# New instruction orders on four engines in the last stage of a two-block gated decoder kernel

## The chip, the cores and the metric

The kernel runs on one core of one Trainium2 chip. Its time is the device time of one execution in microseconds (us); a row of figures is given as the median of several runs. Lower is better. Five engines run their own instruction streams side by side and meet at semaphores: TensorE (PE) multiplies matrices, VectorE (DVE) and ScalarE (ACT) work on rows, GpSimd (POOL) issues the indexed gathers and does a little arithmetic, SyncE (SP) issues most other transfers. An instruction that has to wait holds up everything behind it on its engine.

## The reference, cut to what matters

```
x = x + tanh(g_xattn[0]) * xattn(layernorm(x), ctx, ctx, mask)      # cross attention, 77 keys
x = x + tanh(g_ffn[0])   * moe(layernorm(x))                        # 8 experts, top 2, plus a shared expert
x = x + tanh(g_xattn[1]) * L1_xattn(layernorm(x), ctx, ctx)         # softmax over the queries
x = x + tanh(g_ffn[1])   * L1_ffn(layernorm(x))
# L1_ffn: h = silu(x @ wg.T) * (x @ wu.T);  out = h @ wd.T          # hidden width 768, int weights / 127
```

x is 4 batches of 1024 rows of 256 numbers in float32. `L1_xattn` normalizes its softmax over the 1024 queries of a batch, so a batch has to be complete before its output can be formed.

## The kernel before, in words

Rows are cut into 8 groups `u` of 512 (4 tiles of 128 rows, `GT` = 4), two groups to a batch (`GB` = 2). The first stages (attention, routing, experts) fill the first 420 us. The last stage computes, group by group, the tail of the expert layer, `L1_xattn` and `L1_ffn`, and writes the output. This text calls one pass of `for b in range(B)` a turn; there are four. Turn `b` runs `L1_ffn` of batch `b` (groups `2b` and `2b+1`, called its first and second half here, `c` = 0 and 1) and, woven in, all that batch `b+1` needs before it.

The names in the code, with their engine:

- `up3(b, c, m)` on TensorE: block `m` of six of gate and up products, 8 matmuls into two banks. `down3(b, c, False)` and `down3(b, c, True)`: blocks 0 to 3, then 4 and 5, of the product with `wd`. The first of these calls works on tiles 0 and 1, then waits for the product of block 5 and works on tiles 2 and 3.
- `hidden3` on ScalarE issues for block `m` a silu (L1008, into one of three buffers `sl`), and then the high part `g3h` (L699). On VectorE `hidden3` is the gated product, silu times up (L2155), in place; `low3` is the low part `g3l` (L2160), product minus high part. The next silu in the same buffer waits for that low part. `up3` of block `m` waits for the gated product of block `m-2`, since it writes the same banks.
- For batch `b+1`: `gather` on GpSimd (L624, 8 indexed DMAs per group, two to a tile) fetches expert rows; `x2` on VectorE (L2077) adds them in, 8 instructions per group; `stats3` (L2086, L2089), `rstd3` on GpSimd (L633, L637), `shift3` (L2102) and `norm3` on ScalarE (L961) are the layer norm; `t3` (L1554) transposes, `copy_n3` copies to SBUF, `scores3` (L1562) multiplies with the keys, `score_max` and `softmax3` follow, `out3` (L1571) forms the output, `residual3` adds it, `stats4`, `norm4`, `t4` (L1580), `copy_n4` and `n4_low` make the input of `up3`, and `final` (L2169) forms the result.

The order of work on each engine is written out by hand; there is no scheduler. On GpSimd `paced(b, c, j, m)` issues the gather of tile `j` only once `m` gated products are done. On every engine the order of the code is the order in which work is issued.

## Time and profile before

| | |
|---|---|
| median of 3 runs | 638.63 us (636.67 to 639.14) |
| span of the profiled execution | 657.9 us |
| TensorE busy | 607.1 us, 92% |
| VectorE busy | 443.4 us, 67% |
| ScalarE busy | 363.6 us, 55% |
| GpSimd busy | 250.0 us, 38% |
| mean granted TensorE clock | 0.979 |

The times of the three runs are device times of executions without a profile; the profile is of another execution, whose span is 19.3 us longer than the median. No other time of the profiled execution is recorded beside its span. The four turns of the last stage lie at about 469.9 to 523.1, 523.1 to 571.7, 571.7 to 619.8 and 619.8 to 657.9 us of the span. Busy time on TensorE is the union of modelled matmul times; a back-to-back matmul starts about 0.23 us after the one before but is shown as 0.39 us long, so a gap in the stream of starts is about 0.16 us longer than the idle time that the profile shows.

### The profile page before, as it was taken

To read this page: it belongs to the slowest core of one execution; us is meant where nothing else is said; L and a number is where in the kernel's file an instruction comes from. 1 tells how busy PE (TensorE), PEld (TensorE's weight loads), DVE (VectorE), ACT (ScalarE), POOL (GpSimd) and SP (SyncE) were. 2 spreads that over 40 slices of the span, in tenths; PEclk is the share of its full clock that TensorE was granted. 3 is DMA by queue.
4 is the path that set the end of the run, shared out by engine and by line. 5 is a ranking of instruction groups with operands and counts; after the bars stand their busy time and mean duration, and the time that the engine had idled before them with its cause. 6 is when DMAs were issued, how large, how long until landed. Compare 5 with 4: busy or idle time off the path is not lost.

```text
span 657.9 us, 12684 instructions
## 1 busy us (share of the span) xinstructions
PE 607.1 (92%) x3562; PEld 498.5 (76%) x3562; DVE 443.4 (67%) x1321; ACT 363.6 (55%) x806; POOL 250.0 (38%) x315
## 2 busy tenths in 40 slices
PE   8889999888986999999999999699879989999997
PEld 6667777776755788888888888586757867877886
DVE  3988888864653666666666663467876796866755
ACT  5687778855532555555555543155654674674643
POOL 4345564434352336232323236567442732200000
PEclk9899999988898999999999999899999999999999
DMA  6335664454063953333333317532111331100000
GB/s 199 126 126 180 220 204 160 164 167 143 25 256 120 321 162 106 105 106 105 105 107 105 106 57 260 204 117 71 49 49 48 101 108 48 49 1 32 33 33 33
DMA packets 46657, 77.53 MB, mean 118 GB/s; under 512 B 7604, under 2 KB 31615, under 8 KB 46335
## 3 DMA queue, kind: packets, MB, share of 16 engines
q1 hardware_dynamic: 38521, 57.55, 26.3%
q0 software_dynamic: 7344, 19.14, 8.7%
q8 instruction: 33, 0.54, 0.3%
q14 instruction: 33, 0.27, 0.1%
q10 hardware_dynamic: 726, 0.02, 0.1%
HBM read 44.52 MB, written 32.17 MB: 117 GB/s over the span
## 4 chain that ended last, share of the span: by engine, by line
PE 52%; DVE 18%; issue 9%; ACT 7%; DMA 4%; POOL 4%; another core or an unknown queue 4%; SPq 1%; ACTq 0%; DVEq 0%; POOLq 0%
PE bank L1162 11%; PE bank L1164 10%; PE bank L1163 10%; PE bank L1602 5%; PE bank L1623 3%; PE bank L1624 3%; PE bank L1464 2%; PE bank L1455 2%; DMA rows_by_expert<-n,pos 2%; DVE xa L2077 2%; DVE st L2086 2%; PE bank L1562 2%; DVE sl L2155 1%; DVE xa L2138 1%
## 5 line engine op out<-in xcount | busy, mean ns | idle before, releaser
L582 POOL TENSOR_TENSOR yg<-yg,b 128x256 f32<-128x256 f32 x71 | 52.3, 737 | 115.7 <-ACT yg L699 115.7
L2038 DVE TENSOR_TENSOR hb<-bank,b 128x512 f32<-128x512 f32 x71 | 49.1, 692 | 59.4 <-PE bank L1164 59.1
L536 POOL DMA_INDIRECT rows_by_expert<-n,pos x64 | 65.6, 1025 | 61.2 <-DVE pos L1890 44.7
L1602 PE MATMUL bank<-n4Th,wint 128*128 128x512 f32 x192 | 74.6, 409 | 5.5 <-DVE sl L2155 4.1
L624 POOL DMA_INDIRECT yr<-expert_out,out_row x64 | 66.7, 1042 | 20.4 <-issue 17.4
L699 ACT ACTIVATE hTh<-bank 128x256 fp32r<-128x256 f32 x71 | 27.3, 384 | 82.0 <-PE bank L1464 82.0
L1602 PE MATMUL bank<-n4Tl,wint 128*128 128x512 f32 x192 | 71.9, 395 | 0.0
L699 ACT ACTIVATE g3h<-sl 128x512 fp32r<-128x512 f32 x60 | 37.8, 631 | 45.5 <-DVE sl L2155 32.0
L1162 PE MATMUL bank<-w13h,xTh 128*128 x142 | 56.4, 397 | 0.2 <-DVE xTl L2045 0.2
L1164 PE MATMUL bank<-w13h,xTl 128*128 x142 | 56.0, 394 | 0.0
L1163 PE MATMUL bank<-w13l,xTh 128*128 x142 | 55.8, 393 | 0.0
L1162 PE MATMUL bank<-n2Th,wsh 128*128 128x256 f32 (+1 forms) x128 | 44.3, 346 | 9.2 <-DVE n2Tl L1819 3.3
L1623 PE MATMUL bank<-wint,g3h 128*128 128x256 f32 x192 | 48.2, 292 | 2.4 <-issue 1.4
L1602 PEld LDWEIGHTS bank<-n4Th,wint 128*128 128x128 f32 x192 | 35.4, 188 | 17.8 <-DVE sl L2155 8.6
L2155 DVE TENSOR_TENSOR sl<-bank,sl 128x512 f32<-128x512 f32 x48 | 32.9, 686 | 23.3 <-ACT sl L1008 23.3
L1162 PE MATMUL bank<-w2h,hTh 128*128 x142 | 45.8, 323 | 0.3 <-DVE hTl L2042 0.3
L1624 PE MATMUL bank<-wint,g3l 128*128 128x256 f32 x192 | 46.0, 281 | 0.0
L633 POOL TENSOR_SCALAR ve<-mv 128x4 f32<-128x4 f32 x16 | 6.0, 377 | 102.7 <-DVE mv L2089 97.0
L1602 PEld LDWEIGHTS bank<-n4Tl,wint 128*128 128x128 f32 x192 | 36.0, 188 | 8.0
L1163 PE MATMUL bank<-n2Tl,wsh 128*128 128x256 f32 (+1 forms) x128 | 41.6, 325 | 0.0
L1164 PE MATMUL bank<-n2Th,wsl 128*128 128x256 f32 (+1 forms) x128 | 41.3, 323 | 0.0
L961 ACT ACTIVATE n<-xa,nb,rs 128x256 f32<-128x256 f32 x64 | 34.2, 595 | 10.7 <-DVE nb L2102 10.7
(299 smaller groups left out, 1787.6 us busy)
## 6 DMA issues: line engine op xcount, KB each, us to landing
xg<-rows_by_expert SPq DMA_DIRECT2D x71, 128.0 KB, 2.1
expert_out<-yg SPq DMA_DIRECT2D x71, 128.0 KB, 1.7
stage<-in_wexp SPq DMA_DIRECT2D x24, 256.0 KB
x_shared<-x SPq DMA_DIRECT2D x8, 512.0 KB
xa<-x_shared SPq DMA_DIRECT2D x4, 1024.0 KB
out<-ost SPq DMA_DIRECT2D x8, 512.0 KB, 2.6
xin<-in_x SPq DMA_DIRECT2D x7, 512.0 KB, 5.1
wint<-in_wint POOLq DMA_DIRECT2D x3, 768.0 KB, 10.7
```

The lines of the kernel that those rows point to most:

```text
L536: pool.indirect_dma_start(out=xs, out_offset=bass.IndirectOffsetOnAxis(ap=pos[p][:, k, j:j + 1], axis=0), in_=n2[p][:, j, :], in_offset=No ...
L582: pool.tensor_tensor(yg[s], yg[s], b2[:, bass.ds(e, 1), :].rearrange("p a d -> p (a d)"), ALU.add)\
L624: pool.indirect_dma_start(out=yr[:, c, k, j, :], out_offset=None, in_=ys, in_offset=bass.IndirectOffsetOnAxis(ap=out_row[:, b * GB + c, k, ...
L699: return act.activation(dst, src, ACT.Copy)
L1162: mm(o, ah, bh, start=first, stop=False)
L1163: mm(o, ah, bl, start=False, stop=False)
L1164: return mm(o, al, bh, start=False, stop=final)
L1602: last = mm(bank[:, 2 * (m % 2) + w, :], wt[:, k, m * P:(m + 1) * P], part[c][:, k, :], start=(q == 0 and k == 0), stop=(q == 1 and k == K ...
L1623: mm(bank[:, j, 0:D], g3h[:, k, t], wdv[:, k, :], start=(k == 0), stop=False)
L1624: last = mm(bank[:, j, 0:D], g3l[:, k, t], wdv[:, k, :], start=False, stop=(k == ML - 1))
L2038: tt(hb[p], bank[:, p, :], b13[:, bass.ds(e, 1), :].rearrange("p a n -> p (a n)"), ALU.add)\
L2155: tt(sl3[n % 3], bank[:, 2 * (m % 2) + 1, :], sl3[n % 3], ALU.mult).then_inc(sem("g3_done"), 1)
```

## The change

The same operations are issued with the same operands; some are cut in halves (two tiles, one bank or one group at a time), and the order on four engines is new. Up to the first turn the order of compute instructions is unchanged on every engine. The core of the diff follows; conditions that hold in the first three turns are left out or joined to their line.

```diff
@@ GpSimd
             paced(2, 0, 3, 1)
+            rstd3(0, 4, "n3_done")
             paced(2, 1, 0, 2)
+            rstd3(1, 2, "n4_done")
             paced(2, 1, 1, 4)
-            rstd3(0, 4, "n3_done")
             paced(2, 1, 2, 6)
-            rstd3(1, 2, "n4_done")
+            rstd3(1, 3, "n4_done")
             paced(2, 1, 3, 8)
             paced(3, 0, 0, 9)
-            rstd3(1, 3, "n4_done")
...
             paced(3, 1, 1, 16)
-            rstd3(0, 6, "n3_done")
+            rstd3(1, 4, "n4_done")
             paced(3, 1, 2, 18)
-            rstd3(1, 4, "n4_done")
             paced(3, 1, 3, 20)
             rstd3(1, 5, "n4_done")
+            rstd3(0, 6, "n3_done")
@@ ScalarE: hidden3 is cut into silu3 (the silu) and high3 (the high part); one turn
+                silu3(b, 0, 0)
+                if nxt: norm3(u, first)
+                if b == 0: copy_n4(1, (0,))
+                high3(b, 0, 0)
+                if b == 0: copy_n4(1, (1,))
+                silu3(b, 0, 1)
+                if nxt: norm3(u, second)
+                silu3(b, 0, 2)
+                high3(b, 0, 1)
+                if nxt: copy_n3(u, (0,)); copy_n3(u, (1,))
+                silu3(b, 0, 3)
+                high3(b, 0, 2)
+                if nxt: norm3(u + 1, first); norm3(u + 1, second)
+                silu3(b, 0, 4)
+                high3(b, 0, 3)
...
@@ TensorE, one turn
                 up3(b, 0, 2)
                 t3(u)
-                for m in range(3, ML): up3(b, 0, m)
-                t3(u + 1)
+                up3(b, 0, 3)
+                up3(b, 0, 4)
+                scores3(b + 1, (0,))
+                t3(u + 1)
+                up3(b, 0, 5)
                 down3(b, 0, False)
-                scores3(b + 1)
+                scores3(b + 1, (1,))
                 down3(b, 0, True)
                 up3(b, 1, 0)
                 up3(b, 1, 1)
-                out3(b + 1)
-                for m in range(2, ML): up3(b, 1, m)
+                out3(b + 1, (0,))
+                up3(b, 1, 2)
+                out3(b + 1, (1,))
+                up3(b, 1, 3)
...
@@ VectorE, second half of a turn
                 hidden3(b, 1, 1)
+                residual3(u, (0,))
                 low3(b, 1, 0)
-                residual3(u)
-                stats4(u)
-                x3_read(u)
-                low3(b, 1, 1)
+                residual3(u, (1,))
+                stats4(u)
+                residual3(u + 1, (0,))
                 hidden3(b, 1, 2)
-                residual3(u + 1)
-                shift3(1, u)
+                low3(b, 1, 1)
+                residual3(u + 1, (1,))
+                shift3(1, u)
                 low3(b, 1, 2)
...
                 hidden3(b, 1, 4)
-                shift3(1, u + 1)
                 hidden3(b, 1, 5)
                 low3(b, 1, 4)
+                shift3(1, u + 1)
```

The line numbers in the next rows are those of the version that each is taken from. First VectorE in the first half of the first turn, before, from the gated product of block 1 to that of block 4 (`sl` in and out: gated product; `g3l`: low part; `xa` from `yr`: the adding of gathered rows; `st` and `mv`: statistics; `nb`: shift).

```order
L2155 TENSOR_TENSOR sl_210<-bank,sl_210 128x512
L2160 TENSOR_TENSOR g3l<-sl_209,g3h 128x512
L2077 SCALAR_TENSOR_TENSOR xa_196<-yr,gate_all,xa_196 128x256 x4
L2086 BN_STATS st_221<-xa_196 128x6 x4
L2089 BN_AGGR mv_223<-st_221 128x2 x4
L2155 TENSOR_TENSOR sl_211<-bank,sl_211 128x512
L2160 TENSOR_TENSOR g3l<-sl_210,g3h 128x512
L2102 SCALAR_TENSOR_TENSOR nb_227<-mv_223,rs_229 128x4
L2155 TENSOR_TENSOR sl_209<-bank,sl_209 128x512
L2160 TENSOR_TENSOR g3l<-sl_211,g3h 128x512
L2077 SCALAR_TENSOR_TENSOR xa_197<-yr,gate_all,xa_197 128x256 x4
L2155 TENSOR_TENSOR sl_210<-bank,sl_210 128x512
```

The same place now, again from block 1's product to block 4's:

```order
L2223 TENSOR_TENSOR sl_210<-bank,sl_210 128x512
L2151 BN_STATS st_221<-xa_196 128x6 x4
L2155 BN_AGGR mv_223<-st_221 128x2 x4
L2228 TENSOR_TENSOR g3l<-sl_209,g3h 128x512
L2223 TENSOR_TENSOR sl_211<-bank,sl_211 128x512
L2228 TENSOR_TENSOR g3l<-sl_210,g3h 128x512
L2168 SCALAR_TENSOR_TENSOR nb_227<-mv_223,rs_229 128x4
L2223 TENSOR_TENSOR sl_209<-bank,sl_209 128x512
L2228 TENSOR_TENSOR g3l<-sl_211,g3h 128x512
L2142 SCALAR_TENSOR_TENSOR xa_197<-yr,gate_all,xa_197 128x256 x2
L2223 TENSOR_TENSOR sl_210<-bank,sl_210 128x512
```

The statistics now stand ahead of block 0's low part, the second pass of `x2(3)` has gone ahead of block 1's product, and block 4's product is behind two instructions of `x2(4)` and no longer behind four.

ScalarE at that place before, from the silu of block 1 to that of block 4 (`sl` from `bank`: silu; `g3h`: high part; `n_201`: norm; `n3T`: copy of the transposed norm):

```order
L1008 ACTIVATE sl_210<-bank 128x512
L961 ACTIVATE n_201<-xa_196,nb_227,rs_229 128x256 x2
L699 ACTIVATE g3h<-sl_210 128x512
L1008 ACTIVATE sl_211<-bank 128x512
L699 ACTIVATE g3h<-sl_211 128x512
L699 ACTIVATE n3T<-bank 128x512 x2
L1008 ACTIVATE sl_209<-bank 128x512
L961 ACTIVATE n_201<-xa_196,nb_227,rs_229 128x256 x2
L699 ACTIVATE g3h<-sl_209 128x512
L1008 ACTIVATE sl_210<-bank 128x512
```

And now:

```order
L1013 ACTIVATE sl_210<-bank 128x512
L966 ACTIVATE n_201<-xa_196,nb_227,rs_229 128x256 x2
L1013 ACTIVATE sl_211<-bank 128x512
L704 ACTIVATE g3h<-sl_210 128x512
L704 ACTIVATE n3T<-bank 128x512 x2
L1013 ACTIVATE sl_209<-bank 128x512
L704 ACTIVATE g3h<-sl_211 128x512
L966 ACTIVATE n_201<-xa_196,nb_227,rs_229 128x256 x4
L1013 ACTIVATE sl_210<-bank 128x512
```

Each silu has moved ahead of the high part of the block before it, and the copies of the transposed norm no longer stand behind block 2's high part.

GpSimd from the first turn on, as a difference (`ve` and `rs` are one `rstd3`, 225 and 229 for the norm of `L1_xattn`, 226 and 230 for that of `L1_ffn`):

```order
-L624 DMA yr<-expert_out,out_row 128x256 x6
-L633 TENSOR_SCALAR ve_225<-mv_223 128x4
-L637 TENSOR_TENSOR rs_229<-ve_225,halfpow 128x4
 L624 DMA yr<-expert_out,out_row 128x256 x2
+L633 TENSOR_SCALAR ve_225<-mv_223 128x4
+L637 TENSOR_TENSOR rs_229<-ve_225,halfpow 128x4
+L624 DMA yr<-expert_out,out_row 128x256 x2
 L633 TENSOR_SCALAR ve_226<-mv_224 128x4
 L637 TENSOR_TENSOR rs_230<-ve_226,halfpow 128x4
```

Four gathers (the tiles 0 and 1 of group 5) that were issued ahead of `rstd3(0, 4)` now come behind it, and two of these behind `rstd3(1, 2)` too.

## Rows read from the trace of the kernel before

**Rows 1.** Busy time by turn: PE, PEld, DVE, ACT, POOL, granted clock, DMA share, GB/s
```profile
469.90:523.10 53.20, 47.79 (x259) 37.77 (x258) 40.16 (x101) 31.33 (x58) 24.72 (x26) 1.00 0.17 53
523.10:571.70 48.60, 46.12 (x250) 36.63 (x249) 38.81 (x98) 29.52 (x55) 15.98 (x18) 1.00 0.23 74
571.70:619.80 48.10, 45.70 (x249) 36.49 (x248) 34.24 (x82) 29.33 (x54) 4.49 (x6) 1.00 0.06 23
619.80:657.90 38.10, 34.22 (x193) 29.08 (x191) 19.95 (x30) 14.74 (x26) 0.00 (x0) 1.00 0.11 42
```
**Rows 2.** Groups by line from 469.9 us on: busy us, mean ns, idle before
```profile
L2155 DVE TENSOR_TENSOR sl<-bank,sl 128x512 f32<-128x512 f32 x48 | 32.9, 686 | 23.3 <-ACT sl L1008 23.3
...
L1008 ACT ACTIVATE sl<-bank 128x512 f32<-128x512 f32 x48 | 28.2, 588 | 18.5 <-DVE g3l L2160 10.0 <-PE bank L1602 8.1
```
**Rows 3.** Timeline, TensorE, first turn: start, length, instruction, [idle before, releaser]
```profile
479.87 0.40 PE L1602 MATMUL bank<-n4Th,wint 128*128 128x512 f32 x1
480.10 0.39 PE L1602 MATMUL bank<-n4Tl,wint 128*128 128x512 f32 x1
481.65 0.50 PE L1602 MATMUL bank<-n4Th,wint 128*128 128x512 f32 x1 [1.16 <-DVE sl L2155]
...
483.40 0.39 PE L1602 MATMUL bank<-n4Tl,wint 128*128 128x512 f32 x1
484.50 0.50 PE L1602 MATMUL bank<-n4Th,wint 128*128 128x512 f32 x1 [0.71 <-DVE sl L2155]
...
486.23 0.39 PE L1602 MATMUL bank<-n4Tl,wint 128*128 128x512 f32 x1
486.73 1.10 PE L1554 MATMUL bank<-ident,n 128*128 128x128 f32 x8
489.20 0.38 PE L1623 MATMUL bank<-wint,g3h 128*128 128x256 f32 x1 [1.37 <-issue]
...
491.08 0.28 PE L1624 MATMUL bank<-wint,g3l 128*128 128x256 f32 x1
491.99 0.38 PE L1623 MATMUL bank<-wint,g3h 128*128 128x256 f32 x1 [0.63 <-DVE sl L2155]
...
497.02 0.68 PE L1623 MATMUL bank<-wint,g3h 128*128 128x256 f32 x1
497.54 0.28 PE L1624 MATMUL bank<-wint,g3l 128*128 128x256 f32 x1
```
**Rows 4.** Timeline, VectorE, first turn
```profile
475.36 1.29 DVE L2149 TENSOR_TENSOR n4Tl<-bank,n4Th 128x512 fp32r<-128x512 f32 x2 [1.30 <-ACT n4Th L699]
...
479.35 1.40 DVE L2086 BATCH_NORM_STATS2 st<-xa 128x6 f32<-128x256 f32 x4
...
480.94 0.66 DVE L2155 TENSOR_TENSOR sl<-bank,sl 128x512 f32<-128x512 f32 x1
481.51 0.68 DVE L2160 TENSOR_TENSOR g3l<-sl,g3h 128x512 fp32r<-128x512 f32 x1
...
486.88 1.67 DVE L2077 SCALAR_TENSOR_TENSOR xa<-yr,gate_all,xa 128x256 f32<-128x256 f32 x4 [1.83 <-DMA yr<-expert_out,out_row]
488.46 0.68 DVE L2155 TENSOR_TENSOR sl<-bank,sl 128x512 f32<-128x512 f32 x1
```
**Rows 5.** Chain that ended last: the landing of that gather (start, length)
```profile
484.06 2.79 DMA yr<-expert_out,out_row
```
**Rows 6.** Timeline, GpSimd, first turn
```profile
481.12 0.23 POOL L633 TENSOR_SCALAR ve<-mv 128x4 f32<-128x4 f32 x1 [8.93 <-DVE mv L2089]
...
508.61 0.57 POOL L633 TENSOR_SCALAR ve<-mv 128x4 f32<-128x4 f32 x1 [9.70 <-DVE mv L2089]
```
**Rows 7.** Who waited for whom, TensorE, second turn: us in total, times, longest
```profile
PE bank L1602 <- DVE sl L2155: 1.1, 2, 0.6
PE bank L1554 <- ACT n L961: 0.4, 1, 0.4
PE bank L1623 <- DVE sl L2155: 0.4, 1, 0.4
```

More of the change, by code:

```diff
@@ L1031, in late_high @@
                 copy(lhh[:, m, :], lsil[m % 2]).then_inc(sem("hh_done"), 1)
+            first, second = range(2), range(2, GT)
             late_silu(0, 0)
@@ L1046, in _ @@
             late_silu(1, 2)
-            norm3(0, range(2))
+            norm3(0, first)
             late_high(1, 2)
-            norm3(0, range(2, GT))
+            norm3(0, second)
             late_silu(1, 3)
@@ L1052, in _ @@
             copy_n3(0)
-            norm3(1)
+            norm3(1, first)
+            norm3(1, second)
             late_silu(2, 0)
@@ L1064, in _ @@
             late_high(2, 3)
-            norm4(0)
-            copy_n4(0)
+            norm4(0, first)
+            norm4(0, second)
+            copy_n4(0, (0,))
+            copy_n4(0, (1,))
             for b in range(B):
@@ new lines, in _ @@
+                silu3(b, 1, 1)
+                high3(b, 1, 0)
+                silu3(b, 1, 2)
+                high3(b, 1, 1)
+                high3(b, 1, 2)
+                silu3(b, 1, 3)
+                if nxt:
+                    norm4(u, first)
+                high3(b, 1, 3)
+                if nxt:
+                    norm4(u, second)
+                silu3(b, 1, 4)
+                high3(b, 1, 4)
+                silu3(b, 1, 5)
+                if nxt:
+                    copy_n4(u, (0,))
@@ L1097, in _ @@
+                high3(b, 1, 5)
+                if nxt:
+                    norm4(u + 1, first)
+                if nxt:
+                    copy_n4(u, (1,))
+                if nxt:
+                    norm4(u + 1, second)
+                if nxt:
+                    copy_n4(u + 1, (0,))
+                if nxt:
+                    copy_n4(u + 1, (1,))
         @block.tensor
@@ L2073, in x2 @@
                 for k in ks:
-                    for j in range(GT):
+                    for j in tiles:
                         if k:
@@ L2205, in _ @@
             late_out(0, 1)
-            stats3(0)
+            stats3(0, first)
+            stats3(0, second)
             late_hidden(1, 1)
@@ L2211, in _ @@
             late_hidden(1, 2)
-            x2(1, (0,))
+            x2(1, (0,), first)
+            x2(1, (0,), second)
             late_hidden(1, 3)
@@ L2215, in _ @@
             late_low(1, 3)
-            x2(1, (1,))
-            stats3(1)
+            x2(1, (1,), first)
+            x2(1, (1,), second)
+            stats3(1, first)
+            stats3(1, second)
             late_out(1, 0)
@@ L2223, in _ @@
             late_low(2, 0)
[L2224 removed]
+            x2(2, (0,), first)
+            x2(2, (0,), second)
+            x2(2, (1,), first)
+            x2(2, (1,), second)
             late_hidden(2, 1)
[L2226 removed]
+            stats3(2, first)
+            stats3(2, second)
             late_low(2, 1)
[L2228 removed]
             score_max(0)
@@ L2231, in _ @@
             late_hidden(2, 2)
-            residual3(0)
+            residual3(0, (0,))
+            residual3(0, (1,))
             late_hidden(2, 3)
-            stats4(0)
+            stats4(0, first)
+            stats4(0, second)
             x3_read(0)
@@ L2238, in _ @@
             shift3(1, 0)
-            residual3(1)
-            stats4(1)
+            residual3(1, (0,))
+            residual3(1, (1,))
+            stats4(1, first)
+            stats4(1, second)
             x3_read(1)
@@ L2279, in _ @@
                 if more:
-                    stats3(u + GB)
+                    stats3(u + GB, first)
+                if more:
+                    stats3(u + GB, second)
                 if nxt:
                     score_max(b + 1)
-                final(b * GB)
+                final(b * GB, (0,))
+                final(b * GB, (1,))
                 if nxt:
```

267 lines of the change are left out of this document (164 added, 103 removed).

## The prediction, made before the changed kernel was run

> **What bounds the kernel now.** I read the busy times by turn first, then the waits of TensorE, then the timelines of the four engines beside each other. In the turns the reader sees TensorE busy for 47.8 of 53.2 us, 46.1 of 48.6, 45.7 of 48.1 and 34.2 of 38.1, at a granted clock of 1.00 throughout, and VectorE for 40.2, 38.8, 34.2 and 20.0 [rows 1]. TensorE is the bound, and its matmuls are the same before and after. So the change can win only what TensorE waits, and that is a few us in each of the first three turns. In the last turn nothing is woven in; its view of waits names none for TensorE, and its 3.9 us without work are the tail behind the last matmul. The share of busy time says nothing more: the question is which of the waits end earlier in the new order.
>
> How long TensorE really stands still I read from starts. Back to back, a matmul of 512 columns starts 0.23 us after the one before it (479.87 and 480.10 in [rows 3]), while it is shown 0.39 us long. So each listed wait is 0.16 us longer in truth, and short ones are not listed. In the first half of the first turn, by the rows:
>
> - before block 4: 481.65 - 480.10 - 0.23 = 1.32 us, for the gated product of block 2;
> - before block 5: 484.50 - 483.40 - 0.23 = 0.87 us, for that of block 3;
> - before the transposes of group 3: 486.73 - 486.23 - 0.23 = 0.27 us, for its norm;
> - before the down product: the eight transposes at 486.73 take about 0.8 us, so 489.20 - 487.54 = 1.66 us, for the product of block 4;
> - in the middle of the down product: 491.99 - 491.08 - 0.12 = 0.79 us, for block 5's [rows 3].
>
> Together 4.9 us. The product of block 4 was late because `x2(4)` ahead of it on VectorE waited 1.83 us for a gather [rows 4], which GpSimd could issue only behind `rstd3(0, 3)`, which waited for the statistics of group 3 [rows 6]. From the start of that `rstd3` at 481.12 to the landing at 484.06 + 2.79 = 486.85 are 5.73 us [rows 5, 6].
>
> **The change part by part, first turn, first half.** VectorE waited 1.30 us for both copies of n4 at 475.36 [rows 4]. Now the first copy stands ahead of block 0's high part on ScalarE, which starts this chain about 0.5 us earlier. The statistics of group 3 also no longer wait for block 0's low part, about 0.6 us (back to back a low part takes 0.6; it is shown as 0.68 [rows 4]). They start about 1.1 us earlier, at 478.3 instead of 479.35. The product of block 2 comes behind them and the low part, so it gains only the 0.5: 480.94 becomes about 480.5. TensorE waits 0.9 instead of 1.32 there: 0.45 won. Block 1's product is now behind all of `x2(3)` and ends at 478.4, just when block 3 wants it: nothing lost, 0.1 at most.
>
> Between blocks 4 and 5 TensorE now has half of the scores (about 1.5 us) and the transposes (0.8). That covers the wait for block 3's product: 0.87 won, and the 0.27 before the transposes goes too, since they come later than the norm is done (about 484.0 against 484.9). `rstd3(0, 3)` starts 1.1 us earlier, so the gather lands at 485.8. Then two instructions of `x2(4)` (1.67 us for four [rows 4], so 0.8) and the product of block 4, 0.69 [rows 2], end at 487.3; TensorE reaches the down product at about 487.7. So the 1.66 us go. But three of the six remaining `x2` pairs are now ahead of block 3's low part, which ends at 489.5, and the down product asks for it 1.4 us after its start, at 489.1: 0.4 lost. Block 5's product ends at 490.1, when the middle of the down product is reached: 0.79 won. Scores in two parts cost one more passage from float32 matmuls to others: the first matmul behind the scores takes 0.52 us to the next start where 0.12 is usual (497.02 and 497.54 in [rows 3]). Bounds are 0 (no gap stands ahead of them, and what follows is now a transpose) and 0.40; I take 0.3, near the row. Sum: 0.45 + 0.87 + 0.27 + 1.66 + 0.79 - 0.4 - 0.3 = 3.3 us.
>
> **Second turn, first half.** Listed waits of TensorE are 1.1 in two places (blocks 2 and 5), 0.4 for a norm and 0.4 in the middle of the down product [rows 7]. The wait ahead of block 2 stays: n4's low parts and four instructions of `x2` stand ahead of block 0's product as before. The norm's wait stays too, as `shift3`, two norm pairs and a silu stand in the same order. Block 5's wait (0.55 + 0.16 = 0.7) goes under scores and transposes, the transposes' own small wait (0.27, as in the first turn) goes, and the one in the down product (0.4 + 0.16, say 0.5) goes, since nothing waits for a gather here. Less 0.3 for the scores: 1.2 us. **Third turn**, the same without the last: 0.7 + 0.27 - 0.3 = 0.7 us.
>
> **Second halves of the turns.** Here TensorE hardly waits. `out3` in two parts costs one more passage (0 to 0.4, I take 0.2), and stands so that the residual of one group overlaps the output of the other; VectorE's norm may be 0.3 us earlier. I take nothing for the three halves together; bounds are a loss of 1.2 (0.4 each) and a gain of 1.8 (0.6 each, were the products never late). **Edits at nothing:** the waits moved into functions, the memsets and the smaller calls before the first turn keep their order, so what lies ahead of 469.9 us stays.
>
> **GpSimd.** A `rstd3` now waits for statistics with gathers queued behind it. `rstd3(0, 4)` holds up two gathers of group 5, and `rstd3(1, 2)` two more. Those come at about 507, the last gather of group 5 lands near 518 and is wanted by `x2(5)` near 521; group 6's eight DMAs end near 527, land near 528.5, and are wanted near 531.5. Both have 3 us in hand, which hides them. If that cover went, each us late would be a us of VectorE ahead of a gated product.
>
> The row that bears on port sharing: the tiny `ve` on GpSimd takes 0.23 us beside a gated product, which reads PSUM, and 0.57 us at 508.61, where VectorE runs a low part with two SBUF inputs [rows 6]. The Trainium skill, "SBUF — State Buffer", section "SBUF: two separate sides", says that a VectorE operation with two SBUF inputs and a GpSimd operation that reads SBUF lock each other out of a shared port pair for a whole instruction; by that rule, the trace agrees, 0.34 us are at stake per `rstd3`, which eats into the 3 us and changes no term.
>
> **Sum.** 3.3 + 1.2 + 0.7 = 5.2 us less. The profiled span would go from 657.9 to 652.7. The runs without a profile are 19.3 us shorter than the span; I carry the difference over in us: 638.63 - 5.2 = **633.4 us**.
>
> **Rivals.**
> (1) *More comes back.* If the remaining waits ahead of blocks 2 and 4 (0.9 in the first turn, 0.7 in the others), the low part's 0.4, and the passages (3 x 0.3) go too, and the second halves give 0.3 each: 5.2 + 0.9 + 1.4 + 0.4 + 0.9 + 0.9 = 9.7, less the norm's part: about 9 us, 629.6. For it: halves let work start early everywhere. Against: VectorE has the same sum of work ahead of those products.
> (2) *The waits are only moved.* The gather lands as late as before (then 0.9 of the 1.66 stays), block 1's product, now behind `x2(3)`, holds up block 3 by 0.5, and both kinds of passage cost their full 0.4 (0.1 more in three scores, 0.4 in three outputs): 5.2 - 0.9 - 0.5 - 0.3 - 1.2 = 2.3 us, 636.3. For it: VectorE is 76% busy in the first turn and each late product costs TensorE at once.
> (3) *Slower: the ring of three silu buffers.* Each high part now waits behind the next block's silu, hence for its matmuls, and the low part comes after it; the silu three blocks on waits for that low part. Three blocks are 3 x 8 x 0.235 = 5.6 us. The chain is one block (1.9), silu 0.59 [rows 2], high part about the same, low part 0.68: 3.8 us. So it decides as soon as more than 1.8 us of other VectorE work stands ahead of the low part; statistics take 1.6. It happens at four places in a turn (two `stats3` or `x2`, two `stats4`), and at 0.7 us each in twelve places it takes 8.4 us and leaves 3.2 us of loss: 641.8. Against it: the margins that I find are 0.2 us and more.
>
> **How the numbers follow.** Forecast, a gain of 3.2 to 7: 0.51. Rival 1, beyond 7: 0.13. Rival 2, within 0.5% (3.2 us, about what a measurement here can tell from no change): 0.27. Rival 3: 0.09. Faster by over 0.5% has the first two, 0.64; same 0.27; slower 0.09. The range runs from 630.0 (rival 1 nearly whole) to 638.3 (all of rival 2 down to no gain; of rival 3 nothing); the forecast's own is 631.5 to 635.5.
>
> **What the changed profile would show.** In the first half of the first turn TensorE waits for no product before block 5 nor before the down product, and the sum of its gaps there is 1.3 to 2 us, not 4.9. The gather of tile 3 of group 4 lands 1 us earlier by the matmuls' own time. Turns two and three are 1.2 and 0.7 us shorter, the fourth unchanged. I am wrong if ScalarE's silus show waits for low parts with TensorE idle beside them (rival 3), if `x2(5)` or `x2(6)` wait for a DMA, or if the second halves move by over 1 us either way.

## The result, and the profile after

| | before | after |
|---|---|---|
| median, same chip | 637.65 us (633.96 to 639.14, 4 runs) | 628.00 us (625.35 to 630.61, 4 runs) |
| ratio | | 0.9842 (0.9809 to 0.9874) |
| span of the profiled execution | 657.9 us | 628.9 us (its own time 630.61) |
| mean granted TensorE clock | 0.979 | 0.997 |

Against 637.65 us the ratio is a gain of 10.1 us (8.0 to 12.2). The forecast was 633.4 us with a range from 630.0 to 638.3: the direction is right, the gain is about twice as large, and the time lies below the range. It lies below rival 1 too, which said 629.6.

The spans of the two profiles differ by 29 us, which is no measure of the change: the profile of before comes from an execution some 20 us slower than the timed ones. Most of it lies ahead of the turns, which begin at 469.9 us before and at 449.1 us after. One place of it is a wait on ScalarE's timeline (before, then after); more on it below.

```profile
423.15 0.69 ACT L1024 ACTIVATE sl<-bank,bs 128x512 f32<-128x512 f32 x1 [13.93 <-remote]
```
```profile
403.65 0.69 ACT L1030 ACTIVATE sl<-bank,bs 128x512 f32<-128x512 f32 x1 [7.38 <-PE bank L1213]
```

The turns themselves can be compared, though only with this one execution: no profile of the kernel before exists from an execution of 637 to 638 us. By the windows of the kernel after (columns as in [rows 1], cut at its own turns):

```profile
449.10:497.80 48.70, 46.16 (x258) 37.68 (x257) 39.24 (x101) 31.69 (x58) 19.74 (x22) 1.00 0.16 47
497.80:544.00 46.20, 44.89 (x250) 36.93 (x249) 38.59 (x99) 29.47 (x54) 20.28 (x22) 1.00 0.27 89
544.00:590.30 46.30, 44.98 (x252) 37.02 (x250) 34.17 (x83) 29.47 (x54) 4.49 (x6) 1.00 0.06 24
590.30:628.90 38.60, 34.24 (x194) 29.33 (x192) 20.48 (x31) 14.73 (x26) 0.00 (x0) 1.00 0.11 42
```

VectorE and ScalarE are busy for as long as before within 2.5%. TensorE's idle time fell from 5.4, 2.5 and 2.4 us [rows 1] to 2.5, 1.3 and 1.3. Its busy time fell too, from 47.8, 46.1 and 45.7 us to 46.2, 44.9 and 45.0, although its matmuls are the same: a short wait behind a matmul is shown as busy, as the next section works out. To see where the time went, I measure each half of a turn from the first `up3` matmul of its block 0 to that of the next half, and t4b, the last, to the start of the last matmul. t1a is the first half of turn 1, t1b the second, and so on. The halves in all tables of this text are such differences of two starts, each from one profile.

| half | t1a | t1b | t2a | t2b | t3a | t3b | t4a | t4b |
|---|---|---|---|---|---|---|---|---|
| before | 29.85 | 23.05 | 25.82 | 22.73 | 25.49 | 22.73 | 17.09 | 17.05 |
| after | 26.60 | 22.14 | 24.07 | 22.15 | 24.09 | 22.14 | 17.09 | 16.91 |
| gained | 3.25 | 0.91 | 1.75 | 0.58 | 1.40 | 0.59 | 0.00 | 0.14 |
| forecast | 3.3 | 0 | 1.2 | 0 | 0.7 | 0 | 0 | 0 |

Together 8.6 us. It lies inside the interval of the measured gain; whether the rest, 1.5 us, is real can't be told. In the profiles of this text from chips as fast as this one, the kernels with this change start their first turn anywhere from 444.8 to 450.0 us.

The timeline of TensorE in the first half of turn 1, after:

```profile
459.24 0.40 PE L1660 MATMUL bank<-n4Tl,wint 128*128 128x512 f32 x1
460.27 0.50 PE L1660 MATMUL bank<-n4Th,wint 128*128 128x512 f32 x1 [0.64 <-DVE sl L2223]
460.61 0.40 PE L1660 MATMUL bank<-n4Tl,wint 128*128 128x512 f32 x1
...
462.24 1.88 PE L1618 MATMUL bank<-n3T,kqT 128*77 128x512 f32 x4
463.95 1.04 PE L1608 MATMUL bank<-ident,n 128*128 128x128 f32 x8
464.74 0.48 PE L1660 MATMUL bank<-n4Th,wint 128*128 128x512 f32 x1
...
468.12 0.28 PE L1682 MATMUL bank<-wint,g3l 128*128 128x256 f32 x1
469.00 0.36 PE L1681 MATMUL bank<-wint,g3h 128*128 128x256 f32 x1 [0.59 <-DVE g3l L2228]
```

Of the five waits in [rows 3] one is left, 460.27 - 459.24 - 0.23 = 0.80 us before block 4 (forecast 0.9), and a new one has come, 469.00 - 468.12 - 0.12 = 0.76 us for a low part in the down product (forecast 0.4). Two waits that the forecast doesn't name are in both kernels: 1.04 us before the transposes of n4 in turn 1, and about 0.5 us ahead of each of the first three second halves. Block 5's wait lies under half of the scores and the transposes. The gather that had held up the product of block 4 is no longer felt, though VectorE waits longer for it than in [rows 4] (timeline of VectorE, after):

```profile
465.18 0.88 DVE L2142 SCALAR_TENSOR_TENSOR xa<-yr,gate_all,xa 128x256 f32<-128x256 f32 x2 [2.96 <-DMA yr<-expert_out,out_row]
465.98 0.68 DVE L2223 TENSOR_TENSOR sl<-bank,sl 128x512 f32<-128x512 f32 x1
466.58 1.67 DVE L2142 SCALAR_TENSOR_TENSOR xa<-yr,gate_all,xa 128x256 f32<-128x256 f32 x4
468.16 0.69 DVE L2228 TENSOR_TENSOR g3l<-sl,g3h 128x512 fp32r<-128x512 f32 x1
```

It starts 16.1 us into the turn instead of 16.95, and two `x2` instead of four stand between it and the product. In all four turns this is the only `x2` that shows a wait for a gather.

### The profile page after: what moved, and what is told of

It reads as the page before. It is cut to its first block, busy times and chain, and to the rows that moved or that the text cites. A ratio compares the mean times of both kernels' runs of the same rounds, so it can differ in the third digit from the quotient of the medians.

```text
span 628.9 us, 12725 instructions
## 1 busy us (share of the span) xinstructions
PE 594.8 (95%) x3562; PEld 493.5 (78%) x3562; DVE 442.4 (70%) x1321; ACT 364.0 (58%) x806; POOL 249.2 (40%) x315
## 4 chain that ended last, share of the span: by engine, by line
PE 56%; DVE 12%; issue 8%; ACT 7%; POOL 7%; DMA 7%; SPq 3%; ACTq 0%; POOLq 0%; DVEq 0%
PE bank L1660 11%; PE bank L1211 9%; PE bank L1213 9%; PE bank L1212 9%; POOL yr L624 3%; PE bank L1681 3%; PE bank L1682 3%; DMA rows_by_expert<-n,pos 3%; PE bank L1513 2%; PE bank L1504 2%; POOL rows_by_expert L536 2%; PE bank L1629 2%; DVE xa L2142 2%; DMA stage<-in_wexp 1%; DVE n2Tl L1882 1%
## 5 line engine op out<-in xcount | busy, mean ns | idle before, releaser
L1211 PE MATMUL bank<-n2Th,wsh 128*128 128x256 f32 (+1 forms) x128 | 42.8, 334 | 9.3 <-DVE x L1894 6.8
L2223 DVE TENSOR_TENSOR sl<-bank,sl 128x512 f32<-128x512 f32 x48 | 33.1, 689 | 26.0 <-ACT sl L1013 25.4
L1681 PE MATMUL bank<-wint,g3h 128*128 128x256 f32 x192 | 47.8, 291 | 0.6 <-DVE g3l L2228 0.6
L1013 ACT ACTIVATE sl<-bank 128x512 f32<-128x512 f32 x48 | 28.3, 589 | 30.9 <-PE bank L1660 30.4
L1212 PE MATMUL bank<-n2Tl,wsh 128*128 128x256 f32 (+1 forms) x128 | 40.2, 314 | 0.0
```

The costliest lines, as they stand in the source:

```text
L1211: mm(o, ah, bh, start=first, stop=False)
L1212: mm(o, ah, bl, start=False, stop=False)
L1681: mm(bank[:, j, 0:D], g3h[:, k, t], wdv[:, k, :], start=(k == 0), stop=False)
```

## What the forecast left out

**Cut operations cost TensorE nothing.** I had charged 0.3 us for scores in two parts and 0.2 for outputs in two. By the starts, scores whole take 497.02 - 493.99 = 3.03 us (before), the halves 463.95 - 462.24 = 1.71 and 472.81 - 471.50 = 1.31 us. The outputs whole take 506.86 - 503.60 = 3.26 us, a half 481.05 - 479.51 = 1.54. First before, then after:

```profile
493.99 3.60 PE L1562 MATMUL bank<-n3T,kqT 128*77 128x512 f32 x8
497.02 0.68 PE L1623 MATMUL bank<-wint,g3h 128*128 128x256 f32 x1
...
503.60 3.62 PE L1571 MATMUL bank<-vob,attnT 97*128 97x256 f32 x16
506.86 0.58 PE L1602 MATMUL bank<-n4Th,wint 128*128 128x512 f32 x1
```
```profile
471.50 1.88 PE L1618 MATMUL bank<-n3T,kqT 128*77 128x512 f32 x4
472.81 0.68 PE L1681 MATMUL bank<-wint,g3h 128*128 128x256 f32 x1
...
479.51 1.89 PE L1629 MATMUL bank<-vob,attnT 97*128 97x256 f32 x8
481.05 0.58 PE L1660 MATMUL bank<-n4Th,wint 128*128 128x512 f32 x1
481.48 0.39 PE L1660 MATMUL bank<-n4Tl,wint 128*128 128x512 f32 x1
```

The first step behind outputs is 0.42 us instead of 0.23, and it now comes twice; but the two pieces take 3.08 us where the whole took 3.26, so the sum is the same. The steps one by one tell why. Inside the scores of before each step is 0.43 us, but from the last score to the down product it is 0.03, and the step behind that is the 0.52 us that I had charged as a cost over the usual 0.12. What is too much in one step is missing in the one before it: the last score's own time is recorded one instruction late. There was no cost, with the scores whole or cut.

**Waits too short for the list.** The view of waits names none for TensorE in the second half of turn 2 behind its first matmul. The timeline of before has them:

```profile
561.31 0.40 PE L1602 MATMUL bank<-n4Tl,wint 128*128 128x512 f32 x1
561.85 0.50 PE L1602 MATMUL bank<-n4Th,wint 128*128 128x512 f32 x1
562.19 0.40 PE L1602 MATMUL bank<-n4Tl,wint 128*128 128x512 f32 x1
562.43 0.39 PE L1602 MATMUL bank<-n4Th,wint 128*128 128x512 f32 x1
...
563.60 0.39 PE L1602 MATMUL bank<-n4Tl,wint 128*128 128x512 f32 x1
563.98 1.09 PE L1580 MATMUL bank<-ident,n 128*128 128x128 f32 x8
564.83 0.36 PE L1623 MATMUL bank<-wint,g3h 128*128 128x256 f32 x1
```

Ahead of block 5 the step is 0.54 us instead of 0.23, ahead of the transposes 0.38. A matmul is shown 0.16 us longer than its step, so a wait under that shows as no idle time, and one of 0.3 us shows as 0.15. Turn 1's second half has the same two, and a third of 0.24 us in the middle of its down product. The kernel after has none of these; in turn 2:

```profile
536.41 0.40 PE L1660 MATMUL bank<-n4Tl,wint 128*128 128x512 f32 x1
536.64 1.04 PE L1638 MATMUL bank<-ident,n 128*128 128x128 f32 x8
537.45 0.38 PE L1681 MATMUL bank<-wint,g3h 128*128 128x256 f32 x1
```

**A wait costs more than itself.** The step behind a late matmul is 0.34 us (561.85 to 562.19, and 460.27 to 460.61) where 0.23 is usual. So each wait that goes gives 0.1 us more. With that t2b closes by rows: 0.31 + 0.10 + 0.15 = 0.56 of the 0.58 us.

## The experiments

The result and the runs below are six comparisons, each within one chip, and they fall in two kinds. In three the kernel before takes 637 to 638 us, in three 652 to 655 us, and there both kernels show long waits of ScalarE, most of which no event in the trace ends. I call those chips the second kind. That it is the chip is not shown, since none was used twice; the profile of before, 657.9 us long, has the signs of the second kind too, though the timed executions beside it took 634 to 639 us. A ratio is always to the kernel before on the same chip, and the halves come from one profile each.

### Is each half its own matter?

*The kernel before as it is.* (second kind)

> The kernel before, once more, for a second profile of it. By turns the first profile of before has 52.90, 48.55, 48.38 and 33.98 us from first matmul to first matmul, the changed one 48.74, 46.22, 46.23 and 34.00: 8.6 us less. Theory: the four turns repeat within 0.2 us each, and the 20.9 us by which the first turn started earlier in the changed kernel's profile (449.1 against 469.9 us) belong to the execution that was profiled (granted clock 0.979 against 0.997): the first turn starts here at 449 to 452. Rival: part of the measured gain, 10 us by the ratio, lies ahead of the turns, and the first turn starts here at 454 or later at a clock like the changed kernel's.

652.0 us; halves 29.82, 23.08, 25.82, 22.73, 25.50, 22.73, 17.09, 17.07. They are those of the first table to 0.03 us, on another chip, so the halves are a good measure. But this execution too is of the second kind. Its first turn starts at 462.3 us, at a granted clock of 0.984, and not at 449 to 452 as the theory had it, nor at a clock like the changed kernel's as the rival had it; so whether part of the gain lies ahead of the turns stays open.

*Old second halves on VectorE, ScalarE and TensorE*, first halves new:

```diff
 TensorE, second half of each turn (VectorE, ScalarE likewise)
-                out3(b + 1, (0,))
-                up3(b, 1, 2)
-                out3(b + 1, (1,))
-                up3(b, 1, 3)
-                up3(b, 1, 4)
-                up3(b, 1, 5)
+                out3(b + 1)
+                for m in range(2, ML):
+                    up3(b, 1, m)
```

> The changed kernel with the old order in the second half of each turn on VectorE, ScalarE and TensorE, the new one in the first half and on GpSimd. Theory (waits of 0.3 to 0.6 us too short for the list of waits were in the second halves and I left them out): the second halves take 23.0, 22.7 and 22.9 us again where the changed kernel has 22.1 each, so 2.2 us are lost: turns of about 49.6, 46.8 and 47.0. Rival (the second halves only profit from an earlier start of their work in the first halves): they stay within 0.2 us of 22.1 each, and under 0.6 us is lost.

646.98 us, ratio 0.9924 (0.9899 to 0.9950) to the kernel before on the chip. First halves 26.53, 24.89, 24.08; second 23.06, 23.07, 22.72: where the order is new the new numbers stay (t2a would be 24.1; see below), and where it is old t1b and t3b return to the old numbers. t2b is even 0.34 us longer than in the kernel before, by a wait of 0.24 + 0.10 us in its down product that the kernel before has in t1b alone. So the theory holds: the second halves' own order gives their gain.

*Old first halves*, the same way round:

```diff
 TensorE, first half of each turn (VectorE, ScalarE likewise)
-                t3(u, (0,)); t3(u, (1,))
-                up3(b, 0, 3); up3(b, 0, 4)
-                scores3(b + 1, (0,))
-                t3(u + 1, (0,)); t3(u + 1, (1,))
-                up3(b, 0, 5)
+                t3(u)
+                for m in range(3, ML):
+                    up3(b, 0, m)
+                t3(u + 1)
                 down3(b, 0, False)
-                scores3(b + 1, (1,))
+                scores3(b + 1)
```

> The changed kernel with the old order in the first half of each turn on VectorE, ScalarE and TensorE, the new one in the second half and on GpSimd. Theory (the halves add up): the first halves take 29.9, 25.8 and 25.5 us again where the changed kernel has 26.6, 24.1 and 24.1, so 6.4 us are lost, and the second halves keep their 22.1 each. Rival (the GpSimd order makes the first turn's gather land early by itself): the first turn's first half stays under 28.5 us with the old orders elsewhere.

652.87 us, ratio 1.0016 (0.9991 to 1.0042). First halves 29.82, 29.68, 25.20; second 22.21, 22.14, 22.13. t1a is back at its old length, so GpSimd's new order did not bring the gather early by itself. And t1b's 0.9, t2b's 0.6 and t3b's 0.6 us belong to the second halves' own order, for which I had put nothing. t3a gets 0.3 us of its 1.4 from them too. But t2a is 3.9 us longer than in the kernel before, and that eats the gain of the others.

### Which engine's order?

*Old order on TensorE alone*, everything else new (both pieces above, on TensorE only):

> The changed kernel with TensorE's old order in all turns, the other three engines new. Theory (cover: what counts is that scores, transposes and half outputs stand where TensorE used to wait for a gated product): more than half of the 8.6 us is lost, 4.5 to 7 us; TensorE waits again ahead of blocks 2 and 5 of a first half and before the down product. Rival (what counts is that the products come earlier on VectorE and ScalarE): under 2 us is lost, and the waits for products stay short though nothing covers them.

656.59 us, ratio 1.0072 (1.0048 to 1.0096). Halves 28.30, 22.67, 32.35, 22.66, 24.98, 22.63. Against the kernel after, TensorE's own order is worth 1.70 us in t1a, 0.53 in t1b, 0.51 in t2b, 0.89 in t3a and 0.49 in t3b: half to nine tenths of what each gained, and 4.1 of 6.7 us together. That is under the 4.5 to 7 us of the theory for all halves, but t2a, disturbed, can't be counted; the rival, under 2 us, is out. The rest comes from products that are ready earlier. The view of waits of this kernel for t1a names the wait for block 4's product ahead of the down product again, shown as 1.6 us where it was 1.37 [rows 3]:

```profile
PE bank L1681 <- DVE sl L2213: 1.6, 1, 1.6
PE bank L1638 <- ACT n L966: 0.9, 1, 0.9
PE bank L1660 <- DVE sl L2213: 0.6, 1, 0.6
PE bank L1681 <- DVE g3l L2218: 0.6, 1, 0.6
```

*Old order on GpSimd alone.* The edit is the GpSimd part of the change, undone from `paced(2, 0, 3, 1)` on; its first lines:

```diff
             paced(2, 0, 3, 1)
-            rstd3(0, 4, "n3_done")
             paced(2, 1, 0, 2)
-            rstd3(1, 2, "n4_done")
             paced(2, 1, 1, 4)
+            rstd3(0, 4, "n3_done")
             paced(2, 1, 2, 6)
+            rstd3(1, 2, "n4_done")
...
```

> The changed kernel with GpSimd's old order. Theory (GpSimd's order has slack either way, the other engines make the gain): all halves within 0.2 us of the changed kernel's. Rival (a gather queued ahead of a norm's power now delays that norm): rstd3 of the second norms comes later and the second halves of turns one and two take 0.5 us or more longer.

651.28 us, ratio 0.9941 (0.9905 to 0.9976); halves 26.62, 22.27, 29.55, 22.14, 24.08, 22.14. GpSimd's order moves no half (t2a, 29.55, is disturbed here as in the changed kernel beside it). The 3 us that I had counted in hand for its gathers were enough.

*The same together with old first halves:*

> The changed kernel with the old order in the first half of each turn on VectorE, ScalarE and TensorE, and the old order on GpSimd. With GpSimd's new order turn two's first half took 29.7 us, of which ScalarE stood 5.0 us ahead of a copy of n4 with nothing in the trace to end that wait. Theory (the ten gathers in a row of GpSimd's new order, beside the load of a batch, hold up what ScalarE waits for): with the old order it goes, and turn two's first half takes 25.8 us. Rival (the wait has another cause and stays): 28.5 us or more.

One run, 657.15 us; halves 29.84, 22.29, 30.30, 22.14, 25.20, 22.14, those of old first halves alone but for the disturbed one. That one stays, so GpSimd's new order is not what disturbs it: the theory falls and the rival holds.

### Why is the gain smaller on the second kind of chip?

*The changed kernel as it is*, three more times:

> The changed kernel once more, on a chip whose runs of before stand beside it. Theory (the gain is made in the turns and is the same everywhere): halves of 26.6, 22.1, 24.1, 22.2, 24.1, 22.1, 17.1 us within 0.1 each, and 8.6 us less than before, a ratio of 0.986 to 0.987. Rival (waits that no event of the trace ends, as the 5.0 to 5.6 us on ScalarE ahead of the copies of n4 in two of the mixed kernels, also hit the changed kernel on such a chip): one half is 2 us or more longer and the ratio is over 0.990.

> The changed kernel as it is, as the measure for the three kernels beside it. Both theories expect what it showed on the chip where the kernel before took 655 us: the first half of turn 2 near 30.5 us instead of the 24.07 of its first profile, the wait without an event (some 5 us, ahead of ScalarE's copy of the group-3 transposes) in it, and a stretch of about 7 us at the lower granted clock of TensorE behind it. Where the kernel before takes under 640 us, both expect 24.1 us there and no such wait. Time against the kernel before: 0.996 in the first case, 0.985 in the second.

> The changed kernel as the measure for the other three. On a chip where the kernel before takes 650 us or more: first half of turn 2 near 30.5 us, ratio 0.996; where it takes 638 us: 24.1 us and 0.984.

| chip | before | changed | ratio | t1a | t1b | t2a | t2b | t3a | t3b |
|---|---|---|---|---|---|---|---|---|---|
| second kind | 655.32 | 654.55 | 0.9963 (0.9930 to 0.9995) | 26.61 | 22.22 | 30.55 | 22.15 | 24.08 | 22.13 |
| first kind | 638.06 | 627.30 | 0.9842 (0.9803 to 0.9880) | 26.62 | 22.13 | 24.07 | 22.14 | 24.08 | 22.14 |
| second kind | 654.54 | 652.47 | 0.9952 (0.9933 to 0.9971) | 27.14 | 22.28 | 32.03 | 22.14 | 24.09 | 22.14 |

On the first kind the result repeats to the last digit of the ratio. On the second kind the halves repeat (t1a was 0.5 us longer once) but for one: t2a is 6.5 to 8 us longer, and takes back most of the 8.6. Here are the windows of the first 9.2 us of that half on the first kind, and on the second kind with the 6.9 us behind them (columns as in [rows 1]):

```profile
494.90:504.10 9.20, 8.23 (x40) 6.23 (x39) 8.72 (x24) 6.73 (x13) 7.01 (x8) 1.00 0.81 270
```
```profile
515.50:524.70 9.20, 3.98 (x17) 2.90 (x16) 4.21 (x9) 1.08 (x2) 5.68 (x6) 1.00 0.77 256
524.70:531.60 6.90, 5.48 (x17) 4.60 (x18) 6.07 (x17) 5.16 (x10) 1.59 (x2) 0.51 0.05 20
```

And ScalarE's timeline there, again the first kind and then the second:

```profile
495.15 1.09 ACT L704 ACTIVATE n4Th<-bank 128x512 fp32r<-128x512 f32 x2 [1.71 <-PE bank L1638]
497.01 0.60 ACT L1013 ACTIVATE sl<-bank 128x512 f32<-128x512 f32 x1 [0.78 <-PE bank L1660]
```
```profile
519.72 1.08 ACT L704 ACTIVATE n4Th<-bank 128x512 fp32r<-128x512 f32 x2 [5.81 <-remote]
524.74 0.60 ACT L1013 ACTIVATE sl<-bank 128x512 f32<-128x512 f32 x1 [3.94 <-remote]
```
```profile
515.20 0.38 PE L1638 MATMUL bank<-ident,n 128*128 128x128 f32 x2
515.48 1.20 PE L1660 MATMUL bank<-n4Th,wint 128*128 128x512 f32 x4
516.52 1.09 PE L1660 MATMUL bank<-n4Tl,wint 128*128 128x512 f32 x4
```

The third fence is TensorE's timeline on the second kind. ScalarE stands 5.8 us ahead of a copy whose transposes are recorded at 515.2, and then 3.9 us ahead of a silu that needs the eight matmuls from 515.48 on. "Remote" is all that the view can name; by the code, both wait for results of TensorE. Whether TensorE finished these matmuls where they are recorded, or was held back without a record, the trace can't tell. By the records it then runs out of work, and behind that its granted clock is 0.51 for 6.9 us, the lower of its two levels (1.2 instead of 2.4 GHz), where on the first kind it stays at 1.00. The DMA engines are as busy in one as in the other (0.77 and 0.81 of the time), so more traffic is not what sets the second kind apart.

My theory was that TensorE is held back there because the new order leaves it no gaps. A pause ahead of the place should then help, and one behind it should not:

```diff
                 up3(b, 1, 2)
                 if nxt:
                     out3(b + 1, (1,))
+                if b == 0:      # b == 1 in the second kernel
+                    pe.wait_ge(sem("g3_done"), (b * GB + 1) * ML + 3)
                 up3(b, 1, 3)
```

> The changed kernel with one more wait of TensorE: in turn 1's second half, before block 3, it waits for the gated product of block 2, a pause of about 1.6 to 2.2 us and nothing else moved. Theory (TensorE is held back after a stretch without gaps): the second half of turn 1 is 24 to 24.5 us, the wait without an event is gone or small, the first half of turn 2 is 24.1 to 25.5 us; 2.5 to 4.5 us faster than the changed kernel although it only adds a wait. Rival (transfers): 30.5 us stays and the kernel is 1.6 to 2.2 us slower.

> The same added wait of TensorE in the second half of turn 2, so behind the place of the wait without an event. Both theories expect that wait to stay (first half of turn 2 near 30.5 us where the changed kernel has it) and the second half of turn 2 at 24 to 24.5 us instead of 22.15: 1.6 to 2.2 us slower than the changed kernel. If it is as fast as the pause in turn 1, the place of a pause does not matter and the theory falls.

These two fell on a chip of the first kind, which decides nothing of the theory: 629.33 and 629.01 us against 627.30 for the changed kernel; the half with the pause is 23.05 us instead of 22.13 in each, all others are untouched. So the pause is 0.9 us, less than the 1.6 that I had worked out. Again, on the second kind:

> The kernel with the pause of TensorE in turn 1 again (0.92 us on the chip that does not show the wait without an event). Theory (TensorE is held back after a stretch without gaps): on a chip that shows the wait, the first half of turn 2 falls from 30.5 us to 24.1 to 27 us, and the kernel is 2.5 to 5 us faster than the changed one beside it. Rival (transfers there): 30.5 us stays and it is 0.9 us slower. On a chip without the wait both expect 0.9 us slower.

> The kernel with the pause in turn 2 again. Both theories expect 0.9 us slower than the changed kernel beside it, with the wait without an event in turn 2's first half where the changed kernel has it.

652.88 us, ratio 0.9985 (0.9956 to 1.0013), and 654.69 us, ratio 1.0004 (0.9977 to 1.0031). With the pause ahead t1b is 23.71 and t2a 29.50, with the pause behind 22.28 and 31.03; the changed kernel beside them has 22.28 and 32.03. The wait without an event is there in all three, 7.03 us long with the pause ahead. The pair t1b + t2a is 53.2, 53.3 and 54.3 us, and t2a did not fall to 24 to 27 us, so where the pause stands makes no difference that shows. The theory as I had put it falls. A longer pause was not tried.

*The old second half in turn 1 alone*, since with the second halves of all turns old t2a was 24.9 us on a chip of the second kind; first on all three engines, twice, then on VectorE and ScalarE only:

```diff
 VectorE, ScalarE (and TensorE), second half
+                if b == 0:
+                    # the order of the kernel before
+                else:
                     # the new order
```

> The changed kernel, but the second half of turn 1 alone has the old order on VectorE, ScalarE and TensorE. Theory (the wait without an event is TensorE itself, held back after a long stretch of work without gaps, in front of the lower clock that its records show next): the old order puts its three small waits back ahead of that place, so the second half of turn 1 is 0.9 us longer (22.2 to 23.1) and the first half of turn 2 falls from 30.5 to 24.1 to 25.5; together 4 to 5.5 us faster than the changed kernel on the same chip, ratio about 0.988 to 0.990 to the kernel before. Rival (the wait hangs on transfers, the xa load and the output store that SP issues there, whatever TensorE did before): the half of turn 2 stays at 29 to 32 us and the kernel is 0.9 us slower than the changed one.

> The changed kernel with turn 1's second half old on all three engines, on another chip than e9. Where the kernel before takes 650 us or more: if the wait without an event is called up by what turn 1's second half does, the first half of turn 2 is 24.1 to 25.5 us (e1 had 24.9 with both second halves old) and the ratio is near 0.991; if by turn 2's own order, 29 to 32 us stay and the ratio is near 0.997. On a chip where it takes 638 us: as e9, 0.9 us slower than the changed kernel, and the question stays open.

> The changed kernel with turn 1's second half old on VectorE and ScalarE and new on TensorE. Where the kernel before takes 650 us or more: 24.1 to 25.5 us in turn 2's first half if the order of these two engines calls the wait up, 29 to 32 us if TensorE's new order there is enough. In turn 1's second half both expect 22.5 to 23.1 us.

All three fell on the first kind: 630.12 us, ratio 0.9874 (0.9833 to 0.9916); 630.56, 0.9872 (0.9809 to 0.9935); 628.59, 0.9845 (0.9778 to 0.9912). t1b is 23.06, 23.07 and 22.54 us, all other halves are those of the changed kernel to 0.1 us. The last one is the counterpart of TensorE's old order alone (22.67): of t1b's 0.9 us, TensorE's order and that of the other two give 0.5 and 0.4. What disturbs t2a on the second kind stays open.

### Can it be made better still?

*Three edits at the waits that are left*: the gather of tile 3 of group 4 issued two products earlier, the final sum inside the score maximum, and VectorE's norm shift and transposes moved in turns 2 and 3.

> Four further moves in the changed kernel: the gather of tile 3 of group 4 ahead of rstd3(0, 3); in turns two and three the shift of the next norm ahead of the finals of the turn before, and the last two instructions of the first pass of x2 behind block 0's product instead of ahead of it, with the second transposes behind block 5 again; and the first final of a turn ahead of the small steps after the score maximum. Theory (each moves a wait that the changed kernel still has: 0.8 before the down product in turn one, 0.8 before block 2 and 0.6 before the transposes in turns two and three, 0.4 before each second half): first halves of about 25.4, 22.3 and 22.3 us against 26.6, 24.1 and 24.1, 4.8 us less than the changed kernel. Rival (VectorE has the same work ahead of the norm of the second group, so the wait only moves to its transposes): first halves of turns two and three stay over 23.3.

654.83 us, ratio 0.9976 (0.9950 to 1.0001), second kind. t1a is 25.09 instead of 26.61, a little better than the 25.4 expected; t3a is 24.24 instead of 24.08, where 22.3 was expected, so there the wait is only moved. Without the third edit:

```diff
             gather(2, 0, range(2, 3))
+            pool.wait_ge(sem("g3_done"), 1)
+            gather(2, 0, range(3, 4))
             rstd3(0, 3, "n3_done")
...
-            paced(2, 0, 3, 1)
...
-                    score_max(b + 1)
-                final(b * GB, (0,))
+                    score_max(b + 1, lambda: final(b * GB, (0,)))
+                else:
+                    final(b * GB, (0,))
```

> The changed kernel with two further edits: GpSimd issues the last gather of unit (2, 0) as soon as the first gated product of turn 1 is there, not after the third, and VectorE does the final sum of a turn's first group between the two steps of the score maximum, not behind them. Theory: turn 1's first half is 25.1 us instead of 26.6 (as in the run with both of these and a third edit), turn 3's stays at 24.1, so 1.5 us less than the changed kernel. Rival: the gain is only moved to the next low part, then 26.6 us stays.

651.12 us, ratio 0.9948 (0.9912 to 0.9984), beside 652.47 and 0.9952 of the changed kernel. t1a is 25.08, t3a 23.73: 1.5 us less than the changed kernel, as expected, and 0.35 us less, which was not; and t2a, disturbed, 31.21 to its 32.03. Its view of waits for t1a has no low part any more (compare the 0.76 us above):

```profile
PE bank L1639 <- ACT n L967: 0.9, 1, 0.9
PE bank L1661 <- DVE sl L2225: 0.6, 1, 0.6
```

By the undisturbed halves it is the fastest version. By its whole time it is below both kernels in the median, but the intervals of the two new kernels overlap, so that part is not shown. On the second kind the best ratio of all is that of the old second halves, 0.9924 (0.9899 to 0.9950), since it avoids most of the disturbance in t2a.

## Why the prediction missed

- **What bounds the kernel: right.** TensorE's waits in the first three turns are what the change won; the fourth gave 0.14 us.
- **Turn 1, first half, 3.3 us: right, 3.25, in part by luck.** Most terms hold: block 4 0.52 won (0.45), block 5 and the transposes gone, the down product's 1.66 and 0.79 gone. The low part is a loss of 0.76 (0.4), and the wait ahead of the second half, which I had not counted, grew by 0.1. The 0.3 us for cut scores are 0, and that makes up for the low part.
- **Turn 2, first half, 1.2 us: mis-sized, 1.75.** The waits named there are gone, and the norm's and block 2's stay, as said. Without the 0.3 us for the scores it would have been 1.5; two restarts give 0.2 more.
- **Turn 3, first half, 0.7 us: mis-sized, 1.40.** Besides the 0.3 for the scores and a restart of 0.1, the norm's wait fell from 1.11 - 0.23 to 0.84 - 0.23 us. I had copied turn 2's statement that it stays.
- **Second halves, 0 us: this is the step that failed, 2.08 us.** "Here TensorE hardly waits" was read from a view that lists no wait under 0.3 us or so. The timeline has two in each of them, 0.31 and 0.15 us with 0.10 for the restart, and in turn 1 a third of 0.24 with its own restart, and the new order removes them; with the old order back they return. My own rule, that each wait is 0.16 us longer than shown and short ones aren't listed, stood further up in the same text. The upper bound of 1.8 was too low as well. My sign of being wrong, a move of over 1 us, is met by the three together and by none alone (0.91, 0.58, 0.59).
- **The passages, 0.3 us in each of three first halves: a misread row.** The 0.52 us step was the last score's own time, recorded late. It is no cost that a cut can double.
- **GpSimd, nothing: right.** Undoing its order changes no half. The `ve` of group 3, at its new place at 459.13, takes 0.57 us where it took 0.23 [rows 6], and no half shows that.
- **Carrying the difference over: no harm is seen, but it is not proven.** The turns of before repeat to 0.03 us in a second profile, which is of the second kind as well. The changed kernel's halves are the same on both kinds but for t2a and 0.5 us once in t1a.
- **How the miss of 5.4 us adds up.** 3.4 us lie in the halves (8.6 for 5.2), 1.0 in the base (the kernel before took 637.65 us beside the changed one, and I had started from 638.63), and 1.0 in no half; what that last one is stays open.
- **Rivals.** Rival 1 named what happened: the passages cost nothing and the second halves give. It was too generous for the waits ahead of blocks 2 and 4, which stayed at 0.7 and 0.8 us, and for the low part, and gave the second halves 0.9 where they gave 2.1. It deserved more than 0.13: its passages were costs of mine with the bound 0 beside them. Rivals 2 and 3 didn't occur; no silu waited for a low part with TensorE idle beside it.

## What to carry to other kernels

Where the bounding engine's time is to be predicted, measure a stretch from start to start and compare it with the count of its instructions times their back-to-back step. The difference is all that can be won, and it holds the waits that are too short for a list; here a quarter of the measured halves' gain lay in halves that seemed to have next to none. Cut an operation where a short piece of it can cover a wait: the cut itself was free, and TensorE's share of the change gave over half of what the measured halves gained. And time a change on more than one chip before you believe its size: this one was worth 10 us in two comparisons and 2 to 3 us in two others.

## What the runs showed of the hardware

- Chips differ by more than the change: the kernel before takes 637 to 638 us in three comparisons, 652 to 655 us in three.
- On the slower ones ScalarE waits longer for TensorE at two places: ahead of the turns in all kernels (12.2 to 14.0 us, and 7.4 in every profile of the first kind), and in t2a in every kernel with the new second halves on VectorE and ScalarE, where its instruction starts about 4 to 7 us after the matmuls that it waits for are recorded. After each, TensorE's granted clock is about 0.5 for 3 to 7 us. With the old second halves the wait in t2a was 2.1 us, with no lower clock behind it; in the kernel before there is none. What calls it up is open: TensorE's old order did not remove it, GpSimd's neither, nor a pause of 0.9 us. Whether turn 1's second half alone is to blame was not measured on such a chip.
- The first matmul of 512 columns behind a wait is followed by a step of 0.34 us instead of 0.23.
- The step behind the last score is 0.03 us instead of 0.43, and the next is 0.52 instead of 0.12: a group's last step is recorded one instruction late, and looks like a cost of the change of operands.
